# The query stack of a two-stream decoder kernel comes back as 96 rows, and six rows behind it as a second transfer where they must be zero

## The chip, the cores and the metric

The kernel runs on one core of one Trainium2 chip. The metric is the device time of one execution in microseconds (us); lower is better. A core has a matrix engine (TensorE, PE in the profile), a vector engine (VectorE, DVE), a scalar engine (ScalarE, ACT), GpSimd (POOL), a queue engine that only issues transfers and waits (SyncE, SP), and 16 DMA engines that move the bytes of every transfer.

## The reference

The reference is a decoder of four layers over `x` of shape (8, 256, 128): eight sequences of 256 tokens with 128 features. Each layer adds a self-attention, a cross-attention over `ctx` and a feed-forward part to `x`, so there are twelve blocks, numbered 0 to 11 in the kernel:

```
0 L0_attn   1 L0_xattn   2 L0_ffn
3 L1_attn   4 L1_xattn   5 L1_ffn
6 L2_attn   7 L2_xattn   8 L2_ffn
9 L3_attn  10 L3_xattn  11 L3_ffn
```

Five of them (1, 4, 6, 7, 9) are attentions with 16 heads of 8 features. Cut to what matters here, each computes for every head

```
scores = q @ k.T / sqrt(8)            # 256 x 256, block 4 adds a relative-position term
attn   = normalised weights(scores)   # block 1: squared relu; the others: softmax
out    = attn @ v
```

with masks of different kinds. In blocks 6 and 7 the kernel subtracts the row maxima of the scores before the exponential.

## The kernel before, in words

The eight sequences are two streams (`s`) of four items each (`ITEMS = 4`); item `k` of block `n` has the number `j = n * ITEMS + k`. The two streams share all engines. Each engine's program is a set of generators, one per stream and a second one per stream that runs ahead ("front" work: projections and the stacks below), and a string of turns written out by hand (`TURNS`) fixes in which order each engine takes steps from them. The order of instructions on every engine is therefore fixed; only waits decide when they run. SP's program is one such order too: an instruction on SP that waits holds back everything behind it, of both streams.

A head has only 8 features, and the matrix engine wants many rows. For the five blocks 1, 4, 6, 7 and 9 (`FRONTS`) the kernel splits q and k into bf16 pieces and stacks six combinations of them: `COMBOS = 6` times 8 features is 48 rows for an even head and 48 for the odd head of the pair, so a stack has `AUG = 96` rows for 8 pairs of heads and 256 tokens, 4,096 bytes per row. The pieces lie in SBUF in another layout than the matrix engine needs. They are sent to a DRAM tensor `s.via[k]` and come back in the wanted layout:

- `stack_out` waits until the pieces are cut (`s.cut`), and writes them to `via` in two transfers of 192 KB (`stacks<-region` in the profile). 
- `stack_back` waits until both have landed (`s.stack_out`) and reads the stack into SBUF. For the queries (`q_back`, k = 0) this is one transfer of 102 rows into `qs` or, in odd items, into `qv` or another room (`qs<-stacks`, `qv<-stacks`, 408 KB). For the keys (`k_back`, k = 1) it is two transfers of 48 rows into the two halves of `kz` (`kz<-stacks` or `region<-stacks`, 192 KB each). Block 4 has a third stack (k = 2) of 96 rows with one transfer back into `qv_of` (384 KB).

Rows 96 to 101 of the query tile belong to the subtracted maxima. `via[0]` has six more rows behind its 96; they are written once with zeros by `zero_rows` (`stacks<-qs`, two transfers of 24 KB) and never again. In blocks 6 and 7 the scores are first computed with rows 96 to 101 at zero, then SP writes the (negated) maxima into these rows (L2872 `dma(qs[AUG:AUG + 6, ...], s.mpT, s.m_stack)`, `qs<-mpT`), and the scores are computed again. The key tile holds ones in these rows in blocks 6 and 7, and in the odd items of block 9, which use the room of block 6. In blocks 1 and 4 the key tile holds zeros there.

In every front but block 4's the order on SP is: q out, q back, k out, k back. In block 4 it is: third stack out and back, q out, k out, then q back and k back directly behind each other. Block 4 also sends its relative-position scores through DRAM to shift each row by its own offset (`skew<-region`, `skew_room<-skew`, `P<-skew`, L2829 and L2848).

The matrix engine waits for the stacks in `stacks_in` (L802), and in block 4 in `L1_xattn`: first for the third stack, then for everything. All transfers back raise `s.stack_in` by 16 each. `back_before(j)` is the count that all earlier items have raised; SP itself waits for it before it overwrites `via` (L2693).

Of the kernel before, what the change touches and what calls it, by code (L numbers as in the profile page):

```python
# [32 lines left out]
AUG = COMBOS * 2 * DH  # L33
# [486 lines left out]
def program(nc, dram, where, out):  # L520
# [153 lines left out]
    ITEMS = B // 2  # L674
# [22 lines left out]
    def out_before(j):  # L697
        return before(j, 2, 1)
# [19 lines left out]
    def stacks_of(j):  # L718
        return 3 if j // ITEMS == 4 else 2

    def back_before(j):

        m = FRONT_SEQ.index(j)
        return 48 * m + 16 * min(max(m - ITEMS, 0), ITEMS)

    UNITS = [(f, k) for f in range(FT) for k in range(2)]

# [14 lines left out]
    def tensor_program(e):  # L742
        p = Hand(e, "tensor")
# [58 lines left out]

        def stacks_in(s, j):
            yield
            p.wait_ge(s.stack_in, back_before(j) + 16 * (stacks_of(j) + 1))
            p.wait_ge(s.f_out, out_before(j) + 2)
            p.wait_ge(tables, IDENTB)

# [171 lines left out]
        def L0_xattn(s, b, j):  # L980
            yield from stacks_in(s, j)
            p.wait_ge(s.mask_ready, j % ITEMS + 1)
            yield from attend(s, j, s.maskT_of[j % 2], True)
            yield from finish(s, j, W1["L0x_o"], None)
# [144 lines left out]
        def L1_xattn(s, b, j):  # L1129
            qs, qv, kz, v = s.qs_of[4][j % 2], s.qv_of[j % 2], s.kz_of[4][j % 2], s.v_of[4][j % 2]  # L1130
            yield
            p.wait_ge(s.stack_in, back_before(j) + 16)
            p.wait_ge(s.f_out, out_before(j) + 2)
            p.wait_ge(place_sem, 64)
# [36 lines left out]
            for h in range(H + 7):  # L1171
                if h < H:
                    yield from shift(h)
                now = h - 5
                if 0 <= now < H:
                    yield
                    p.wait_ge(s.stack_in, back_before(j) + 64)
                    p.clear(s, "S0")
                    for t in range(TOK):
                        o = s.S0[:, t * S:(t + 1) * S]  # L1180
                        mm(o, qs[:, now // 2, t * 128:(t + 1) * 128], kz[:, now % 2, now // 2, :], True, False)
                        i = mm(o, identb[:, :], L1x_mask[:, t, :], False, True)
                    i.then_inc(s.to_vector, 1)
                    p.fill(s, "S0", s.heads_out)
                if now - 2 >= 3 and (now - 2) % 4 == 3:
                    yield from weigh(now - 2)
                if 0 <= now - 1 < H:
                    yield from turn(now - 1)
                yield
# [219 lines left out]
        def L2_attn(s, b, j):  # L1409
            yield from stacks_in(s, j)  # L1410
            p.wait_ge(scalar_tables, BANDS)
            yield from score_maxima(s, j, bands[:, 0:2, :], 96, 160)
            yield from put_maxima(s)
            yield from attend(s, j, bands[:, 2:4, :], False, 96, 160)
            yield from finish(s, j, P["L2a_o"], RW["L2a_ob"])

        def L2_xattn(s, b, j):
            yield from stacks_in(s, j)
            p.wait_ge(s.mask_ready, ITEMS + j % ITEMS + 1)
            yield from score_maxima(s, j, s.mask_of[j % 2], 0, S)  # L1420
            yield from put_maxima(s)
            yield from attend(s, j, s.maskT)
            yield from finish(s, j, P["L2x_o"], RW["L2x_ob"])
# [1252 lines left out]
    def sync_program(e):  # L2676
        d = Hand(e, "sync")

        def dma(dst, src, sem):
            d.e.dma_start(dst, src).then_inc(sem, 16)  # L2680
# [19 lines left out]
        def stack_back(s, j, k, dsts, clean):  # L2700
            yield
            d.wait_ge(s.stack_out, d.now(s.stack_out))
            d.wait_ge(skew_zero, 160 if j < 2 * ITEMS else 288)
            d.wait_ge(consts_sem, QV_ZERO[s.n])
            d.wait_ge(s.rooms_clean, clean)
            rows_back = s.via[k].rearrange("(r m) -> r m", m=PAIRS * S)
            at = 0
            for dst in dsts:
                n = dst.shape[0]
                dma(dst.rearrange("p i s -> p (i s)"), rows_back[at:at + n], s.stack_in)  # L2710
                at += n

        def q_back(s, j):
            yield from stack_back(s, j, 0, [s.qs_of[j // ITEMS][j % 2][0:AUG + 6]], 0)

        def k_back(s, j):
            yield from stack_back(s, j, 1, [s.kz_of[j // ITEMS][j % 2][HALF * par:HALF * (par + 1), par] for par in range(2)],
# [2 lines left out]
        def front(s, b, j):  # L2720
# [15 lines left out]
            if n == 4:  # L2736
                yield
                d.wait_ge(place_sem, 64)
                yield from stack_out(s, j, 2)
                yield from stack_back(s, j, 2, [s.qv_of[j % 2][0:AUG]], ROOMS[4][1] if j % 2 else 0)  # L2740
                yield from stack_out(s, j, 0)
                yield from stack_out(s, j, 1)
                yield
                d.wait_ge(s.heads_out, H * (ITEMS + k))
                d.wait_ge(s.stack_in, back_before(j) + 16)
                yield from q_back(s, j)
                yield from k_back(s, j)
            else:
                yield from stack_out(s, j, 0)
                yield from q_back(s, j)  # L2750
                yield from stack_out(s, j, 1)
                yield from k_back(s, j)
# [246 lines left out]
```

## Time and profile before

| | |
|---|---|
| runs of the kernel | 2109.3, 2112.57, 2112.61 us; median 2112.57 us |
| span of the profiled execution, first to last instruction | 2089.2 us |
| profiled execution's own time | not recorded; the median of the runs is 23.4 us more than the span |
| PE busy / DVE / ACT / POOL | 1735.3 / 1437.8 / 1036.7 / 461.8 us |
| mean share of the 16 DMA engines | 35.9% hardware queues, 1.4% GpSimd's queue |
| mean granted clock of the matrix engine | 0.929 of full |

The times of single instructions and transfers come from one profiled execution. "Busy" is the time in which an engine ran at least one instruction. The chain of waits is followed back from the last instruction: at each step to whatever released it.

### The profile page before, as it was taken

Reading aid. Unit: us, or ns where it says so; the run is one execution under the profiler, and the core shown is the slowest. Engines: PE = TensorE matmul, PEld = TensorE weight load, DVE = VectorE, ACT = ScalarE, POOL = GpSimd, SP = SyncE. Lnnn points to the kernel's source line nnn. Section 1 sums busy time; section 2 is a strip of 40 time slices with the busy share of each in tenths; the row PEclk is TensorE's granted clock in tenths of the full one; section 3 lists DMA queues with packets and bytes.
Section 4 is the critical chain, followed back from the end, with each engine's and each line's share of the span. In section 5 each row is a group of like instructions: output and inputs, shape, how many; then the busy total and the mean of one; then the engine's idle time right before and its main releaser. Section 6 shows DMA issues by size and latency. Waiting matters only on the chain.

```text
span 2089.2 us, 39934 instructions
## 1 busy us (share of the span) xinstructions
PE 1735.3 (83%) x14536; PEld 1346.3 (64%) x14536; DVE 1437.8 (69%) x4894; ACT 1036.7 (50%) x2588; POOL 461.8 (22%) x448
## 2 busy tenths in 40 slices
PE   6588999999998477778999688899978966774886
PEld 5455687777766355556888576766647865553785
DVE  6688624777877477688988766777875456567743
ACT  3277524666765456657433354445533444541443
POOL 3300110000002000000455400000165554413452
PEclk9899999999999689899999899999988989985998
DMA  5234068000000878878200323323205643322456
GB/s 179 72 82 116 19 217 255 1 1 1 1 1 12 261 207 239 231 204 235 82 1 1 88 72 91 86 70 81 64 25 168 198 138 95 91 75 105 133 179 203
DMA packets 210603, 228.95 MB, mean 110 GB/s; under 512 B 15508, under 2 KB 178732, under 8 KB 209768
## 3 DMA queue, kind: packets, MB, share of 16 engines
q1 hardware_dynamic: 205416, 216.10, 35.9%
q0 software_dynamic: 4992, 10.30, 1.4%
q8 instruction: 116, 1.90, 0.4%
q14 instruction: 79, 0.65, 0.1%
HBM read 130.96 MB, written 94.98 MB: 108 GB/s over the span
## 4 chain that ended last, share of the span: by engine, by line
PE 47%; DVE 22%; DMA 13%; ACT 6%; POOL 5%; issue 4%; SPq 2%; DVEq 0%; ACTq 0%; POOLq 0%
PE banks L746 41%; DMA stacks<-region 3%; ACT P L1512 3%; PE banks L1061 3%; DMA back<-mask,block_to 2%; SPq L2680 2%; POOL sorted L2568 2%; DVE region L1918 2%; DMA skew<-region 2%; DVE P L1838 2%; DVE negm L1849 2%; DVE route L1838 1%; DVE P L2090 1%; ACT region L1512 1%; DVE region L1838 1%
## 5 line engine op out<-in xcount | busy, mean ns | idle before, releaser
L2504 POOL TENSOR_TENSOR norms<-norms,consts 128x2 f32<-128x2 f32 x112 | 81.7, 731 | 1235.5 <-DVE norms L1842 1235.2
L1512 ACT ACTIVATE P<-P,negm 128x256 f32<-128x256 f32 x512 | 240.7, 498 | 118.6 <-DVE negm L2110 64.6
L1512 ACT ACTIVATE P<-banks 128x512 f32<-128x512 f32 (+2 forms) x392 | 187.8, 511 | 158.7 <-PE banks L746 157.0
L1849 DVE TENSOR_REDUCE negm<-banks 128x2 f32<-128x512 f32 (+1 forms) x264 | 148.7, 590 | 31.8 <-PE banks L746 28.6
L746 PE MATMUL banks<-kz,qs 128*128 128x256 bf16 (+1 forms) x512 | 124.7, 279 | 33.6 <-DMA kz<-stacks 16.3
L1512 ACT ACTIVATE region<-banks 128x384 f32<-128x384 f32 (+4 forms) x221 | 108.7, 506 | 77.1 <-PE banks L746 56.5
L746 PE MATMUL banks<-xnT,region 128*128 128x256 f32 x544 | 139.0, 389 | 3.6 <-ACT xnT L1512 3.5
L746 PE MATMUL banks<-bands,identb 128*128 128x160 bf16 (+1 forms) x768 | 140.2, 244 | 0.0
L746 PE MATMUL banks<-region 64*128 64x256 f32 (+6 forms) x922 | 126.3, 364 | 9.0 <-ACT region L1512 3.3
L746 PE MATMUL banks<-qs,kz 128*128 128x256 bf16 (+2 forms) x512 | 113.1, 264 | 22.1 <-DMA kz<-stacks 8.4
L746 PE MATMUL banks<-qv,region 128*128 128x256 bf16 (+2 forms) x512 | 112.7, 262 | 15.6 <-ACT P L1512 13.3
L746 PE MATMUL banks<-kz,region 128*128 128x256 f32 x512 | 121.7, 384 | 4.0 <-DVE skew_room L1838 2.8
L2583 POOL DMA_INDIRECT back<-mask,block_to x92 | 89.4, 972 | 107.9 <-DVE mask L2338 99.2
L746 PEld LDWEIGHTS banks<-xnT,region 128*128 128x128 f32 x544 | 99.2, 193 | 21.8 <-ACT xnT L1512 7.6
L746 PEld LDWEIGHTS banks<-kz,region 128*128 128x128 f32 x512 | 95.6, 191 | 19.9 <-DVE skew_room L1838 4.9
L1838 DVE TENSOR_TENSOR P<-P 128x512 f32<-128x512 f32 (+1 forms) x136 | 84.6, 662 | 33.4 <-ACT P L1512 32.5
L746 PEld LDWEIGHTS banks<-region 128*128 128x128 f32 (+3 forms) x922 | 80.4, 162 | 36.8 <-issue 16.4
L746 PE MATMUL banks<-P,region 128*32 128x256 f32 (+6 forms) x1408 | 91.7, 321 | 9.9 <-ACT P L1512 3.7
L746 PE MATMUL banks<-region,identb 128*128 128x256 bf16 x384 | 99.9, 287 | 0.0
L2110 DVE CUSTOM_DVE_ANT_0 P<-banks,region 128x256 f32<-128x256 f32 x256 | 92.6, 418 | 9.4 <-PE banks L746 9.4
L746 PE MATMUL banks<-region,qv 128*128 128x256 bf16 (+2 forms) x384 | 78.7, 267 | 23.7 <-ACT region L1512 9.8
L1153 PE MATMUL banks<-perm,P 128*128 128x128 f32 x512 | 81.8, 289 | 17.5 <-DVE region L2160 9.1
(288 smaller groups left out, 4462.0 us busy)
## 6 DMA issues: line engine op xcount, KB each, us to landing
stacks<-region SPq DMA_DIRECT2D x178, 192.0 KB, 3.0
sorted<-qs SPq DMA_DIRECT2D x4, 4160.0 KB
skew<-region SPq DMA_DIRECT2D x64, 256.0 KB, 4.0
qs<-stacks SPq DMA_DIRECT2D x24, 408.0 KB
kz<-stacks SPq DMA_DIRECT2D x48, 192.0 KB
skew<-region SPq DMA_DIRECT2D x64, 128.0 KB, 3.3
skew_room<-skew SPq DMA_DIRECT2D x32, 256.0 KB, 3.8
P<-skew SPq DMA_DIRECT2D x32, 256.0 KB, 3.6
```

The lines of the kernel that those rows point to most:

```text
L746: return p.e.matmul(o, lhsT, rhs, start=start, stop=stop)
L1061: i = p.e.transpose(s.T[:, k * S + t * 128:k * S + (t + 1) * 128], s.P[:, n // 2 % 2, n % 2, t, k * 128:(k + 1) * 128], ident)
L1153: m = p.e.transpose(s.T[:, k * S + t * 128:k * S + (t + 1) * 128], s.P[:, i % 2, 0, t, k * 128:(k + 1) * 128], ident)
L1512: return a.e.activation(o, i, f, **kw)
L1838: return v.e.tensor_tensor(o, a, b, op)
L1849: return v.e.tensor_reduce(o, a, AX, op, negate=negate)
L1918: step(v.e.tensor_copy(dst, t.unsqueeze(1).to_broadcast([128, dst.shape[1], S])))
L2110: m = v.e.tensor_tensor_reduce(Pq[:, t, :], s.bank[par][:, t * S:(t + 1) * S], rel[:, h, 128 - 128 * t:128 - 128 * t + S], -1.0, 3.0e38, A ...
L2504: g.e.tensor_tensor(room[:, :, 0], room[:, :, 0], pows[:, :], ALU.pow).then_inc(done, 1)
L2568: g.e.indirect_dma_start(s.sorted_x[w][:, :], place(s, item, k, t), s.own_rows[:, item, t, :], None).then_inc(s.moved[item % 2], 16)
L2583: g.e.indirect_dma_start(s.back[:, :], to, s.block_y[:, n % 2, :], None).then_inc(s.stored[n % 2], 16)
L2680: d.e.dma_start(dst, src).then_inc(sem, 16)
```

## The change

The query stack comes back as 96 rows everywhere. In blocks 6, 7 and 9 a second transfer follows it at once, for rows 96 to 101. In blocks 1 and 4 rows 96 to 101 of the query tile are no longer written. The counts follow: an item raises `s.stack_in` by 48 in block 1 and by 64 in the four others.

```
     def back_before(j):
         m = FRONT_SEQ.index(j)
-        return 48 * m + 16 * min(max(m - ITEMS, 0), ITEMS)
+        return 48 * m + 16 * max(m - ITEMS, 0)
...
         def stacks_in(s, j):
             yield
-            p.wait_ge(s.stack_in, back_before(j) + 16 * (stacks_of(j) + 1))
+            p.wait_ge(s.stack_in, back_before(j) + (48 if j // ITEMS == 1 else 64))
...
         def q_back(s, j):
-            yield from stack_back(s, j, 0, [s.qs_of[j // ITEMS][j % 2][0:AUG + 6]], 0)
+            qs = s.qs_of[j // ITEMS][j % 2]
+            yield from stack_back(s, j, 0, [qs[0:AUG]] + ([qs[AUG:AUG + 6]] if j // ITEMS in (6, 7, 9) else []), 0)
```

`stack_back` issues one transfer for each tile of its list, one behind the other, with no wait between them.

## Rows read from the trace of the kernel before

**Rows 1.** The page: span, first line of busy time, chain by engine.

```profile
span 2089.2 us, 39934 instructions
...
PE 1735.3 (83%) x14536; PEld 1346.3 (64%) x14536; DVE 1437.8 (69%) x4894; ACT 1036.7 (50%) x2588; POOL 461.8 (22%) x448
...
PE 47%; DVE 22%; DMA 13%; ACT 6%; POOL 5%; issue 4%; SPq 2%; DVEq 0%; ACTq 0%; POOLq 0%
```

**Rows 2.** Busy time by window; last three: PE clock, DMA share, GB/s.

```profile
672.00:990.00 318.00, 232.20 (x1898) 160.75 (x1898) 233.83 (x807) 186.63 (x435) 15.69 (x19) 0.86 0.81 227
1150.00:1490.00 340.00, 296.69 (x3368) 229.11 (x3367) 243.16 (x606) 162.47 (x360) 30.90 (x36) 0.95 0.31 79
...
777.40:783.40 6.00, 5.19 (x30) 2.92 (x22) 0.97 (x3) 1.07 (x3) 0.00 (x0) 0.50 0.84 240
```

**Rows 3.** The page's DMA issues: count, KB each.

```profile
qs<-stacks SPq DMA_DIRECT2D x24, 408.0 KB
...
qv<-stacks SPq DMA_DIRECT2D x4, 384.0 KB
```

**Rows 4.** DMA view of 1156:1162 us, 40 slices of 0.15 us: busy tenths, GB/s.

```profile
DMA  0000003703132232334424244424210000004999
GB/s 0 0 0 0 0 0 82 82 27 55 55 55 82 109 137 109 164 164 164 164 109 164 109 164 164 164 109 164 109 55 27 0 0 0 0 0 106 201 177 174
```

**Rows 5.** DMA view of 750:755 us, 40 slices of 0.125 us: GB/s.

```profile
GB/s 172 135 205 242 348 336 234 156 238 369 393 328 238 139 164 98 164 197 66 164 328 360 393 360 393 328 66 33 33 0 0 0 0 0 0 70 193 188 180 172
```

**Rows 6.** DMA busy tenths of 771:785 us, then of 940:952 us, 40 slices each.

```profile
DMA  3078997958768689999999999999444445658879
...
DMA  8986999999958899999994599999998444436999
```

**Rows 7.** Pieces of the chain of waits: start us, us, what.

```profile
171.90 6.14 DMA kz<-stacks
...
709.22 7.21 DMA skew<-region
...
777.39 6.00 DMA skew<-region
...
784.85 6.84 DMA skew<-region
...
863.52 5.57 DMA P<-skew
...
944.90 5.88 DMA skew_room<-skew
...
1191.30 4.74 DMA qs<-mpT
...
1212.20 2.48 DMA qs<-mpT
...
1288.79 6.10 DMA qs<-mpT
```

**Rows 8.** SP's issues in order of time: start us, us, what.

```profile
1288.44 0.26 SPq L2680 DMA_DIRECT2D qv<-stacks  x1
1288.79 0.79 SPq L2680 DMA_DIRECT2D qs<-mpT  x1
...
1744.37 0.27 SPq L2680 DMA_DIRECT2D qs<-stacks  x1
1747.92 1.24 SPq L2680 DMA_DIRECT2D stacks<-region  x2
1751.48 0.78 SPq L2680 DMA_DIRECT2D kz<-stacks  x2
```

**Rows 9.** Issues that touch stacks: ns min/median/max, first and last start us.

```profile
L2680 SPq DMA_DIRECT2D stacks<-qs x2: 402/536/670, 35.7 to 39.5; - x2
```

**Rows 10.** The chain at 1751 us: start us, us, what.

```profile
1751.83 3.33 DMA kz<-stacks
```

**Rows 11.** PE's waits: us in total, times, longest us.

```profile
PE banks L746 <- DMA kz<-stacks: 24.7, 6, 11.5
```

## The prediction

> **What bounds the kernel now.** I read the page first: the chain of waits is matrix engine 47%, vector engine 22%, transfers 13%, and the matrix engine is busy for 1735.3 of 2089.2 us [rows 1]. So the whole is bound by the matrix engine's fixed order, and a transfer counts only where the chain runs through one. The windows show where that is [rows 2]: in block 4 (672 to 990 us) the 16 DMA engines are busy for 0.81 of the time, in blocks 6 and 7 (1150 to 1490 us) for 0.31. The list of issues says what the change can touch: 102-row transfers of 408 KB [rows 3]. There are 40 of them (24 into `qs`, 16 into `qv`), of which 24 belong to blocks 6, 7 and 9 and 16 to blocks 1 and 4.
>
> Then the transfer itself. From 1156 to 1162 us the 102 rows travel alone [rows 4]. For 25 slices of 0.15 us, 3.7 us in all, the share stays at 2 to 4 tenths and the rate does not pass 164 GB/s. Six of 16 engines are 0.375, so the rows lie on about six engines, 17 rows each: 4,096 bytes at 164 / 6 = 27 GB/s are 0.15 us a row, 2.6 us for 17. The trace also has the shape of the new transfer: block 4's third stack is 96 rows, 384 KB, at four places into `qv` [rows 3] and at four into another room. One is under way at the end of the busy part of 750 to 755 us, and it runs at 328 to 393 GB/s [rows 5], the rate of all 16 engines. 393 KB at 360 GB/s are 1.1 us, 6 rows per engine. So 96 rows need 1.5 us less than 102, and 11 rows or 1.65 us less on each of the six engines that carried 17.
>
> **What the change removes.** The gain is that work of other transfers no longer queues behind 17 rows on six engines. In the DMA view this shows as a tail: the share falls to 4 tenths for some time while the last rows drain. Such a tail ends just where a chain piece ends. The piece that starts at 777.39 us and takes 6.00 us ends at 783.4, after a tail of 2.1 us (780.8 to 782.9); the one at 944.90 ends at 950.8, as a tail of 1.5 us ends [rows 6, 7]. Five chain pieces of block 4 and one of block 1 read this way; their tails are 1.2 to 2.5 us, the longest before the end of the piece at 709.22. Spread over 16 engines the same bytes take 6/16 of a tail, so 10/16 of it goes.
>
> - Block 4, no second transfer there: pieces at 709.22, 777.39, 784.85, 863.52 and 944.90 us [rows 7]. Tails of 2.5, 2.1, 1.8, 1.5 and 1.5 us make 9.4 us; 10/16 are 5.9 us.
> - Block 1, no second transfer either: the piece at 171.90 us has a tail of 1.25 us, so 0.8 us. At the start both streams send 17 rows within 2.3 us of each other; I put 1 us there, by the same measure. Together 1.8 us.
> - Blocks 6 and 7: three pieces are the 24 KB of maxima, `qs<-mpT`, and their six rows go to the same few engines. Undisturbed this takes 2.48 us; right behind 102-row transfers it takes 4.74 and 6.10 us [rows 7]. For the first, two such transfers were issued 5 us before; they lose 20 of 34 rows, 3.0 us, more than the 2.3 us of excess, so I take 2. For the second one transfer is issued 0.35 us ahead [rows 8]: 10 of 17 rows go (six stay, one is the new transfer's), 1.5 us.
> - Block 9: chain pieces there land in 2.9 to 3.3 us, as undisturbed ones do. Nothing to win.
>
> The sum is 5.9 + 1.8 + 3.5 = 11.2 us if every piece passes its gain on.
>
> **What it adds.** 24 transfers of six rows, 24 KB. On the DMA engines one row each on six of them, 0.15 us: already in the counts above. On SP an issue each. The nearest row is the same shape in the other direction, `stacks<-qs`, 402 to 670 ns; a 102-row issue takes 0.26 to 0.27 us when SP is not crowded; the dearest neighbour is the six-row `qs<-mpT`, which walks 48 source rows, at 0.79 us [rows 8, 9]. I take 0.3 us, since the new transfer has six whole rows like the first two and not the source of the third. All 24 would be 7.2 us (6.2 to 19). But what stands behind them on SP? At 1744.37 us nothing: the next issue comes 3.5 us later because its pieces are not cut [rows 8]. Nearly all places in block 9 and most in 6 and 7 look like this. At 1288.44 us the maxima's transfer stands right behind, and it is on the chain: 0.3 us there, and about as much at two or three places more, of which I count one. Cost on the chain 0.6 us (0.3 to 4).
>
> The wait of `stacks_in` for blocks 6, 7 and 9 is for 64 and not 48. Its last part is still the key stack, which is issued some 7 us after the query's [rows 8], so the second transfer has landed long before. Two transfers behind each other to one semaphore exist already: the keys' pair at 1751.48 us is landed 3.33 us after the first was handed over [rows 10], so the second of a pair costs a few tenths and not a landing of its own.
>
> The Trainium skill speaks against the change here: its page "DMA: Bandwidth & Descriptors", section "Rules for kernel authors", says to coalesce small transfers, as under 64 KB mostly overhead is paid, and the section on one DMA's anatomy gives 2.0 us of fixed cost each. By that the 24 additions would cost 48 us if each were waited for alone. The trace disagrees for pairs issued together, by its 3.33 us for the keys' two.
>
> **The sum.** 11.2 less 0.6 is 10.6 us. That is too much to expect: the chain follows one path, while two streams share the engines in fixed order, and with one wait shorter the matrix engine meets the next. Two facts bear on how much survives. The matrix engine really stands still for the key stacks only in part: 24.7 us over six times, of which 11.5 at 708 us, where the DMA engines are full and a tail is short [rows 11]. And while the chain runs through a transfer in block 4 the matrix engine is often at work for the other stream: busy 5.19 of 6.00 us from 777.4 us [rows 2]. I take 0.6 of it, between all and a quarter: 6.5 us. The change lies wholly inside the span: 2089.2 would become 2082.7, and the median of 2112.57, which is 23.4 us above the span, 2106.0 us, 0.3% less.
>
> **The rivals.**
>
> *All of it arrives.* The shifting loop of block 4 is a ring of transfers and exponentials in which each stream waits for its own last lane, so nothing else need take a delay's place: minus 10 to 15 us, about 2100. For it: the ends of the tails and of the pieces match. Against it: the busy matrix engine in the same windows.
>
> *Hidden.* The tails delay only the stream that is behind, and the vector engine (22% of the chain) is next at once. Then a quarter or less of 10.6 us survives, minus 0 to 3, about 2110.5. For it speaks again 5.19 of 6.00 us busy; against it that the granted clock is 0.50 there [rows 2], the lower level of 1.2 GHz, after stretches in which the engine stood waiting.
>
> *The clock.* In block 4 the mean granted clock is 0.86 and it falls to 0.50 for stretches of 6 to 12 us [rows 2]. An earlier arrival changes which gaps it follows. One such stretch more or less is 3 to 6 us of matrix work either way. This moves each of the other cases and gives the ends of the range.
>
> *SP's issues: the slower side.* The added issues cost as much as the maxima's, 0.79 us, and most stand on the chain, because SP's order is shared: what one stream issues late, the other waits for. 24 times 0.79 is 19 us, less the 6.5 us gained: plus 12, 2125. It needs more than (6.5 + 4.2) / 24 = 0.45 us of chain per added issue to come out slower at all. Against it stands the gap behind nearly each of them [rows 8].
>
> *The change does not do what it says:* 96 rows also go to few engines. The 328 to 393 GB/s of the same shape exclude it [rows 5].
>
> **Chances.** Forecast (minus 4.3 to minus 10) 0.45; all of it 0.17; hidden, within 4.2 us, 0.29; slower by SP's issues 0.04 and by the clock 0.05. A measurement of this kernel tells about 0.2%, 4.2 us, from no change (its three runs lie within 3.3 us). So faster 0.62, same 0.29, slower 0.09. The range reaches over most of the first two cases and the hidden one, to 2097 and 2114.
>
> **What the profile after would show.** A query transfer alone at 300 GB/s or more for about 1.1 us; no tails of 4 tenths in block 4 except where six-row transfers run; the pieces near 777, 785, 863 and 945 us shorter by about 1 us each; `qs<-mpT` behind a query transfer at about 3 and 4.5 us; SP's issues of 24 KB near 0.3 us; 24 more of them. If tails go and the end of block 4 (near 990 us) does not come earlier, the hidden case holds. If block 4 gains and the blocks 6 to 9 give it back, SP's issues are the cause. The prediction would be wrong above all by the surviving share, 0.6, and by the clock.

## The result

| | us |
|---|---|
| before, four runs | 2109.3 to 2115.41, median 2112.59 |
| changed, four runs | 2091.02 to 2096.54, median 2094.55 |
| ratio, 95% interval | 0.9913 [0.9898, 0.9927] |
| forecast | 2106.0, range 2097 to 2114 |

The changed kernel is 18 us faster, 0.87%. The direction was right, but the gain is nearly three times the forecast and the time lies below the range.

The profile after shows a puzzle first. Its page:

```profile
span 2094.5 us, 39958 instructions
## 1 busy us (share of the span) xinstructions
PE 1745.7 (83%) x14536; PEld 1356.6 (65%) x14536; DVE 1438.9 (69%) x4894; ACT 1035.9 (49%) x2588; POOL 461.7 (22%) x448
```

Its span is 5.3 us longer than that of before [rows 1], although its runs are 18 us shorter. The profiled execution of the changed kernel took 2096.31 us at a span of 2094.5: only 1.8 us lie around a span. By that, an estimate, the first profile of before was not an execution of 2112 us with 23.4 us around it, as I had read it, but one of about 2091 us, quicker than each of its four timed runs. Below, the same kernel is profiled again and spans 2103.4 us. Spans of single profiles can't carry a difference of 0.9% here. Sections of them can, where they agree.

The trace of every kernel here holds 5,232 records of the vector engine, those that the page does not count as busy among them, in the same order. So the records with the numbers 445, 1,561, 2,435, 3,560 and 4,523, counted from nought, mark the same work in each. They cut the execution at 240, 672, 990, 1490 and 1850 us of the first profile: start and block 1; blocks 2 and 3; block 4; blocks 5 to 7; blocks 8 and 9 and what lies between; the last. Durations of these sections in us, worked out from the traces of all 14 profiles:

```
                       1      2,3    4      5-7    8,9    10,11
before, first          240.2  431.7  318.1  500.0  360.1  238.8
before, again  (e1)    242.0  431.7  318.6  503.4  363.1  244.5
changed, first         237.7  431.7  306.8  498.3  366.4  253.3
changed, again (e2)    238.4  431.7  311.7  500.7  366.4  247.6
e3  96 in 1, 4         236.4  431.7  305.3  500.5  364.2  244.1
e4  split in 6, 7, 9   240.5  431.7  321.0  500.4  361.4  242.1
e5  96 in 4            241.2  431.7  306.7  505.0  364.1  248.2
e6  96 in 1            236.9  431.7  316.1  504.7  364.5  247.6
e7  112 everywhere     236.6  431.7  312.2  501.1  365.2  246.2
e8  96 or 112          235.6  431.7  305.5  499.3  364.1  244.2
e9  100 in 4           240.2  431.7  310.8  506.9  367.4  249.0
e10 111 in 4           241.9  431.7  339.5  499.5  363.8  248.4
e11 V as 64 + 32       237.5  431.7  308.8  499.0  363.1  249.5
e12 V as 68 + 28       236.6  431.7  320.6  499.0  366.4  246.6
```

Blocks 2 and 3 have none of these transfers and take 431.7 us in all 14. Block 4 separates: 316.1 to 321.0 us in the four profiles with 102 rows there, 305.3 to 311.7 in the five with 96 rows and nothing else changed in it. The last section, which the change doesn't touch, spreads from 238.8 to 253.3 us, and the first profile of before has the shortest of all, as it has of blocks 8 and 9 (360.1 us). Between the two first profiles the first four sections gain 15.5 us together, and the last two lose 6.3 and 14.5. That is the puzzle solved as far as it concerns the change: the quick end of one profile, from block 8 on, hid a gain in block 4.

Block 4 in the changed kernel, as a window (last three: clock, DMA share, GB/s):

```profile
669.40:976.20 306.80, 228.30 (x1898) 159.28 (x1898) 233.48 (x807) 186.42 (x436) 15.81 (x19) 0.87 0.84 235
```

Against [rows 2] the same 1,898 matrix instructions are busy for 228.3 us instead of 232.2, and the engine is idle for 78.5 us instead of 85.8. The 11.2 us between these two profiles are 7.3 us of idle time and 3.9 us of busy time, with a granted clock of 0.87 and 0.86. The DMA share rose, from 0.81 to 0.84: hardly fewer bytes in less time, and on more engines at once.

The transfer alone, in slices of 0.15 us from 1142 us (two issues, 96 rows and six):

```profile
DMA  0000000029791549999120000000000000000006
GB/s 0 0 0 0 0 0 0 0 82 164 109 300 27 164 164 410 437 437 382 27 55 27 0 0 0 0 0 0 0 0 0 0 0 0 0 0 0 0 0 133
```

By the GB/s it takes 14 slices from first to last, 2.1 us, where the 102 rows took 25 [rows 4], and reaches 437 GB/s where they stopped at 164. In block 4 the stretches of 4 tenths have shrunk to a slice or two (763 to 777 us, then 917 to 929 us; compare [rows 6]):

```profile
DMA  0998992000989994999999789999999999999989
...
DMA  9999999999999898999999999999940067995999
```

Over the whole of block 4, cut into slices of 0.25 us, the packets in the traces fill 0.30 to 0.45 of the 16 engines for 18.75 to 20.5 us in the four profiles with 102 rows, and for 5.25 to 6.75 us in the five with 96.

The list of issues, and SP's issues in order of time in block 9:

```profile
qs<-stacks SPq DMA_DIRECT2D x24, 384.0 KB
...
qs<-stacks SPq DMA_DIRECT2D x12, 24.0 KB
qv<-stacks SPq DMA_DIRECT2D x12, 24.0 KB
```

```profile
1733.83 0.68 SPq L2680 DMA_DIRECT2D qs<-stacks  x2
1737.84 1.25 SPq L2680 DMA_DIRECT2D stacks<-region  x2
```

Both issues together take 0.68 us where one took 0.27 [rows 8], and the next thing SP does still comes 3.3 us later. The issue of six rows by itself takes 0.33 us in the median.

The chain of waits after, in block 4 and at two transfers of maxima:

```profile
705.25 5.35 DMA skew<-region
712.17 6.03 DMA skew<-region
...
785.83 4.79 DMA skew_room<-skew
...
852.79 5.41 DMA P<-skew
...
917.49 6.23 DMA kz<-stacks
929.69 5.73 DMA skew<-region
...
1198.60 2.48 DMA qs<-mpT
...
1276.27 4.28 DMA qs<-mpT
```

Most of these pieces are not those of [rows 7]: the chain takes other transfers. SP's order is the same in both kernels, so each piece of [rows 7] has its counterpart after, and the raises of its semaphore in the traces say when it landed. From issue to landing in us, with the second profile of each kernel (e1 and e2) beside the first:

| piece of before | before, e1 | after, e2 | difference of the means | forecast |
|---|---|---|---|---|
| block 1, 171.90 | 6.14, 6.10 | 3.87, 3.72 | -2.3 | -0.8 |
| block 4, 709.22 | 7.21, 6.97 | 5.35, 5.45 | -1.7 | -1.6 |
| 777.39 | 6.00, 6.02 | 3.98, 3.66 | -2.2 | -1.3 |
| 784.85 | 6.84, 6.83 | 2.39, 2.24 | -4.5 | -1.1 |
| 863.52 | 5.57, 6.69 | 5.41, 4.55 | -1.2 | -0.9 |
| 944.90 | 5.88, 6.37 | 6.71, 6.94 | +0.7 | -0.9 |
| maxima, 1191.30 | 4.74, 6.38 | 2.67, 2.69 | -2.9 | -2 |
| maxima, 1288.79 | 6.10, 6.15 | 4.28, 4.35 | -1.8 | -1.5 |

The 2.48 us at 1198.60 is the counterpart of the undisturbed piece at 1212.20 [rows 7]; the first maxima's counterpart was issued at 1178.16 us and is no longer on the chain. The matrix engine's waits for the key stacks fell from 24.7 us over six [rows 11] to:

```profile
PE banks L746 <- DMA kz<-stacks: 15.1, 4, 9.3
```

### The profile page after: what moved, and what is told of

Same layout as the page of the kernel before. It is cut to its first block, busy times and chain, and to the rows that moved or that the text cites. A ratio compares the mean times of both kernels' runs of the same rounds, so it can differ in the third digit from the quotient of the medians.

```text
span 2094.5 us, 39958 instructions
## 1 busy us (share of the span) xinstructions
PE 1745.7 (83%) x14536; PEld 1356.6 (65%) x14536; DVE 1438.9 (69%) x4894; ACT 1035.9 (49%) x2588; POOL 461.7 (22%) x448
## 4 chain that ended last, share of the span: by engine, by line
PE 49%; DVE 22%; DMA 11%; ACT 7%; issue 6%; POOL 2%; SPq 2%; another core or an unknown queue 0%; DVEq 0%; ACTq 0%; POOLq 0%
PE banks L746 42%; ACT P L1512 4%; PE banks L1061 3%; DMA stacks<-region 3%; SPq L2680 2%; DVE region L1918 2%; DMA back<-mask,block_to 2%; DVE P L1838 2%; DVE negm L1849 2%; DVE P L2090 1%; ACT region L1512 1%; DVE route L1838 1%; DVE region L2160 1%; DVE region L1838 1%; PE banks L1153 1%
```

## The experiments

Ratios are to the kernel before on the same chip, with 95% intervals. Its median was 2109.84 us beside e1 to e4, 2107.74 beside e5 to e8 and 2114.05 beside e9 to e12.

**Is the gain real, and is the first profile typical?** e1 is the kernel before, e2 the changed one, both unchanged.

> The kernel before, unchanged, timed against itself and profiled again. Its first profile spans 2089.2 us although its runs take 2109 to 2115 us, while the changed kernel's profile spans 2094.5 us and its runs take 2091 to 2097. Theory A (the imbalance of the 102-row transfers costs real time, and the first profile shows an execution that is quicker than the usual one): the runs take about 2112 us again and a profile of the same chip spans about 2110 us. Rival B (the kernel before has two ways to run, 2091 and 2112 us, and the change only alters how often each comes): some runs or the profile come out near 2091 us. Rival C (the two sets of runs stood under different conditions): ratio to itself 1.000 either way.

> The changed kernel once more beside the kernel before on one chip. A: 2094 us, ratio 0.991. B: some runs near 2110 us. C: ratio nearer to 0.997, as predicted.

e1: 2110.19 us, ratio 1.0001 [0.9981, 1.002], profile 2103.4 us; its 12 runs lie between 2102.57 and 2113.21. e2: 2090.89 us, ratio 0.9903 [0.9873, 0.9933], profile 2096.7 us. The gain stands, and rivals B and C fall: the runs of before spread over 17 us without two groups (23 of them, 2098.74 to 2115.94), and none came as low as the 2091 us of its first profile. As A said, that execution was quicker than the usual one; why is not known beyond the two sections in which it was, blocks 8 and 9 and the last.

**Which blocks?** e3 and e4 halve the change, e5 and e6 halve e3. The lists `NARROW` and `SECOND` name the blocks with 96 rows and with the second transfer:

```
+            n, qs = j // ITEMS, s.qs_of[j // ITEMS][j % 2]
+            yield from stack_back(s, j, 0, [qs[0:AUG] if n in NARROW else qs[0:AUG + 6]]
+                                  + ([qs[AUG:AUG + 6]] if n in SECOND else []), 0)
# e3: NARROW (1, 4), SECOND ()      e4: both (6, 7, 9)
# e5: NARROW (4,),   SECOND ()      e6: NARROW (1,), SECOND ()
```

The counts in `back_before` and `stacks_in` follow the two lists.

> Only blocks 1 and 4 get the 96-row transfer (16 of 40), blocks 6, 7 and 9 keep one transfer of 102 rows. By my sum block 1 and 4 hold 7.7 of 11.2 us: with the whole at minus 18 us this gives about minus 12 us, ratio 0.994. Rival (the gain sits where the six-row maxima stand behind the query transfer, blocks 6 and 7): minus 3 us or less.

> Only blocks 6, 7 and 9 are changed: 96 rows and the six-row transfer behind them; blocks 1 and 4 keep 102 rows. If the parts add up, this and the run with blocks 1 and 4 alone sum to about minus 18 us, with minus 6 us here (ratio 0.997). If the added issues cost on the chain, it is 0 or slower here. Rival: minus 12 us or more here, the gain is in the maxima.

> Block 4 alone gets 96 rows (8 of 40 transfers). Aligned by the vector engine's instruction count, the profiles put 11 us of the gain into block 4. Theory (real relief of the full DMA engines): minus 13 to 16 us in the runs, ratio 0.993, and a gain of about 11 us between 672 and 990 us of the profile. Rival (the gain is made of small shifts everywhere and not of block 4): minus 3 us.

> Block 1 alone gets 96 rows (8 of 40). My prediction had 1.8 us at best there; the profiles say about 3. Both: ratio 0.998 to 0.999, span up to 240 us shorter by 2 to 4 us. Rival (an early gain is handed on and grows in block 4 by another alignment of the streams): minus 8 us or more.

| | us | ratio | less than before |
|---|---|---|---|
| e3, blocks 1 and 4 | 2089.95 | 0.9910 [0.9881, 0.9939] | 19.0 |
| e4, blocks 6, 7, 9 | 2105.58 | 0.9986 [0.9965, 1.0007] | 3.0 |
| e5, block 4 | 2095.88 | 0.9939 [0.9915, 0.9962] | 12.9 |
| e6, block 1 | 2104.14 | 0.9983 [0.9971, 0.9995] | 3.6 |

(The last column is one less the ratio, times the median of before.) The parts add up within their intervals: 12.9 + 3.6 + 3.0 is 19.5, the whole in e2 20.5. Block 4, a fifth of the transfers, has two thirds of the gain. I had expected 12 us of e3 and 6 of e4. In blocks 6, 7 and 9 the interval reaches from 7.4 us of gain to 1.5 of loss, so these runs do not show that the change does anything for the time there.

**Is it the number of engines or the number of bytes, and do the issues cost?** e7 takes the other way to 16 engines: 112 rows, more bytes, one transfer. e8 does so only where the zeros are needed.

```
-        self.via = nc.dram_tensor(f"stacks{n}", (3, (AUG + 6) * PAIRS * S), BF16).ap()
+        self.via = nc.dram_tensor(f"stacks{n}", (3, (AUG + 16) * PAIRS * S), BF16).ap()
...
-            yield from stack_back(s, j, 0, [s.qs_of[j // ITEMS][j % 2][0:AUG + 6]], 0)
+            yield from stack_back(s, j, 0, [s.qs_of[j // ITEMS][j % 2][0:AUG + 16]], 0)     # e7
+            n = j // ITEMS                                                                   # e8
+            yield from stack_back(s, j, 0, [s.qs_of[n][j % 2][0:AUG + (16 if n in (6, 7, 9) else 0)]], 0)
...
-            dma(s.via[0, AUG * PAIRS * S:]..., s.qs[0:6]..., skew_zero)
+            dma(s.via[0, AUG * PAIRS * S:]..., s.qs[0:16]..., skew_zero)
```

> All 40 query transfers carry 112 rows (96, the six, and ten more rows of zeros): seven rows on each of 16 engines, one transfer, no added issue, but 448 KB where 408 KB were. If the count of engines is the cause: as fast as the changed kernel, 2091 to 2094 us, a little slower in block 4 for 16 more rows. Rival (fewer bytes and rows are the cause): no gain or slower than before.

> 96 rows in blocks 1 and 4, 112 rows in one transfer in blocks 6, 7 and 9. It has the gain of blocks 1 and 4 and no added issue. If the six-row transfers cost something in the changed kernel: 2 to 4 us faster than it, 2088 us. If not: the same within the noise.

e7: 2090.67 us, 0.9920 [0.9894, 0.9946]. 10% more bytes per transfer than before, and all of the gain within the interval: it is not the bytes. e8: 2087.59 us, 0.9916 [0.9890, 0.9942]. Its median is the lowest of all kernels here, but its interval is nearly the changed kernel's, so the 24 added issues cost nothing that can be seen, and e8 is an equal, not a better version. These intervals are 11 us wide: the 0.6 us that I had forecast for the issues is far below what they could show.

**How does the cost grow?** e9 and e10 change block 4's query transfer alone, to 100 and to 111 rows (the room behind `via` as in e7).

```
+            n = j // ITEMS
+            yield from stack_back(s, j, 0, [s.qs_of[n][j % 2][0:111 if n == 4 else AUG + 6]], 0)    # e9: 100
```

> Only block 4's query transfer is changed, to 100 rows, 400 KB. If such a transfer costs the rows of its fullest engine: 100 rows lie on 10 engines with 10 rows each, against 17 (102 rows) and 6 (96 rows, minus 11.9 us in the runs and 10.4 in the profiles). 7 of 11 rows of relief: minus 7 to 8 us, ratio 0.9965. Rival (it is the whole or nothing: all 16 engines or not): 0. Rival (bytes: 2 of 6 rows fewer): minus 4 us.

> Block 4's query transfer carries 111 rows, 444 KB, which lie on three engines with 37 rows each: 20 more on the fullest than 102 rows have. By the same slope, 1.1 us per row, plus 22 us in the runs, ratio 1.010, all of it between 672 and 990 us. Rival (a transfer of the query lies beside other waits and only its 9% more bytes count): within 3 us of the kernel before. Sharper than the slope if the three engines become the bound of block 4.

e9: 2106.24 us, 0.9962 [0.9947, 0.9976]: 8.0 us less, expected 7 to 8. e10: 2134.03 us, 1.0096 [1.0071, 1.0122]: 20.3 us more, expected 22. The engines' counts in the expectations are those by which the Trainium skill, page "DMA: Bandwidth & Descriptors", section "Why a DMA increments its semaphore by 16 and not by 1", splits a transfer: over the largest number up to 16 that divides its outermost size, so 16 for 96 and 112, 10 for 100, 6 for 102, 3 for 111. No view names the engine of a packet, but the traces confirm the counts in another way: they hold every raise of a semaphore by a transfer. In each of block 4's eight items `s.stack_in` goes up by 64, in 64 raises with 96 or 112 rows, 59 with 100, 55 with 102 and 52 with 111. The third stack and the two key transfers make 48 of them. The query's is left with 16, 11, 7 and 4: one for each engine, and one more for the rest of the 16 where the engines are fewer. Likewise e12's two parts of 68 and 28 rows leave 20, which is 5 and 15.

The time follows the row count of the fullest engine that this gives. The last column is the difference, divided by the difference in rows and by eight transfers:

| rows | on the fullest engine | block 4, us | against 102 rows | per row and transfer |
|---|---|---|---|---|
| 96 | 6 | 307.2 (mean of five) | -11.3 | 0.128 |
| 100 | 10 | 310.8 | -7.7 | 0.138 |
| 102 | 17 | 318.5 (mean of four) | | |
| 111 | 37 | 339.5 | +21.0 | 0.131 |

One row takes 0.15 us on one engine by [rows 4], so 0.85 to 0.92 of each row stands in block 4's time. 112 rows (e7, seven on each) should give 308.2 and have 312.2 in one profile, which is as far off as the five of 96 rows lie from each other. The same holds for the one profile of 100 rows: 310.8 us lies inside the 305.3 to 311.7 of 96. Its runs exclude the rival of no gain (5.1 to 11.2 us less), but not that 100 rows are as good as 96, for e5's interval is 8.0 to 17.9.

In e10 the chain goes through the transfers that queue behind the long one, and they are long (the first of these, `stacks<-region`, is on the chain of before too, with 7.23 us):

```profile
700.37 11.03 DMA stacks<-region
713.27 9.96 DMA kz<-stacks
...
795.79 9.52 DMA P<-skew
...
878.05 9.39 DMA P<-skew
...
946.63 10.25 DMA kz<-stacks
```

and its block 4 as a window shows what a mean hides:

```profile
673.60:1013.10 339.50, 234.51 (x1898) 165.00 (x1898) 233.84 (x807) 187.12 (x436) 15.81 (x19) 0.83 0.77 214
```

The DMA share is the lowest of the three, 0.77, in the kernel that suffers most from its transfers; the matrix engine stands idle for 105.0 us. The tail of three engines shows: the packets fill 0.2 to 0.3 of the 16 engines for 29 us of block 4, where the nine profiles with 96 or 102 rows have 3.5 to 5.75.

**Does it need to be the query's transfer, and what does an issue cost there?** e11 and e12 are the changed kernel with block 4's third stack in two parts. The counts in `back_before` and in three waits follow (80 for 64, 32 for 16).

```
-                yield from stack_back(s, j, 2, [s.qv_of[j % 2][0:AUG]], ROOMS[4][1] if j % 2 else 0)
+                yield from stack_back(s, j, 2, [s.qv_of[j % 2][0:64], s.qv_of[j % 2][64:AUG]], ...)   # e11
+                yield from stack_back(s, j, 2, [s.qv_of[j % 2][0:68], s.qv_of[j % 2][68:AUG]], ...)   # e12
```

> The changed kernel, with block 4's third stack brought back as 64 and 32 rows, all 16 engines each, six rows per engine as before: eight more issues on SP and nothing else. Theory: an issue beside other work costs nothing that can be seen or at most 0.3 us each, 0 to 2.4 us over the changed kernel, ratio to the kernel before 0.991 to 0.992. Rival (a second transfer costs a landing of its own, 2 us): plus 16 us, ratio 0.998.

> The same with 68 and 28 rows: 68 rows lie on four engines with 17 rows each, 28 on 14 with two each. 13 more rows on the fullest engines of a transfer that the matrix engine waits for, eight times, about 2 us each: up to plus 15 us over the run with 64 and 32, by the slope of 1.1 us per row plus 14. Rival (the imbalance matters only for transfers queued behind the query's): plus 3 us or less.

e11: 2094.27 us, 0.9910 [0.9889, 0.9932], where the changed kernel has 0.9903 in e2: eight more issues cost nothing seen, and a landing of its own is excluded. e12: 2100.02 us, 0.9935 [0.9911, 0.9959], so 5.7 us over e11; the two intervals overlap. Block 4 of its profile is 11.8 us longer, 320.6 against 308.8, and 8.9 longer than the longest of the five with an even split (311.7). The direction is as expected, same bytes, same issues, other rows per engine; of the size, 14 us expected, the runs show less than half and the profile most. One profile each and this spread don't settle which.

The third stack is waited for directly. Waits of the matrix engine in block 4, e12:

```profile
PE banks L746 <- DMA qv<-stacks: 12.2, 2, 10.9
...
PE banks L912 <- ACT OTp L1512: 9.2, 6, 6.4
```

and e11:

```profile
PE banks L746 <- DMA kz<-stacks: 9.7, 2, 9.0
PE banks L746 <- DMA qv<-stacks: 9.3, 1, 9.3
```

The waits for the third stack have grown by 2.9 us in total and those of L912, 4.7 us in e11, by 4.5. Where the rest of the 11.8 us stands these lines don't show.

## Why the prediction was wrong

**Right: what the transfer does.** 102 rows on six engines, 96 on 16, 1.65 us less on each of the six. The raises of the semaphore and the four row counts (0.13 us per row, against 0.15 from [rows 4]) bear it out. That a transfer of six rows behind it is cheap was right too: 0.33 us per issue (0.3 forecast), time to spare behind it on SP in block 9, nothing measurable in e7 and e8. The advice of the Trainium skill, page "DMA: Bandwidth & Descriptors", section "Rules for kernel authors", to coalesce small transfers was no reason against the change here. The 2.0 us of fixed cost that the prediction took from the same page stand in its section "Anatomy of one DMA — SWDGE (gpsimd) path", so for transfers that GpSimd issues and not SP; 24 times that did not show. The maxima's two transfers, forecast at about 3 and 4.5 us, took 2.67 and 4.28.

**Wrong: the size of block 4's term.** "Five chain pieces", their visible tails, "10/16 of it goes": 5.9 us, and after the factor of 0.6 some 3.5. Measured are 11.3 us in the profiles and 12.9 in e5's runs. Two steps failed. The first is the count. I took 9.4 us of tails, those at the ends of five pieces of the chain; 19.4 us of such stretches stand in block 4 with 102 rows and 6.0 with 96. So 13.4 us of them went, 1.7 for each of the eight transfers, which is the 1.65 us of my own text. The product of the two, 13.2 us, I never made, and 0.86 of it arrived. The second is the factor: 10/16 of the 13.4 us would be 8.4, and the block gained 11.3. Why it gained more than the tails give by that factor is not shown; the shorter busy time of the matrix engine, 3.9 us of the 11.2, may be part of it. The table of counterparts says the same: of the five pieces one was over in 2.3 us instead of 6.8, where I had 1.1 us of gain, and one did not become shorter at all. Nor do pieces of one chain bound a term: the second profile of the same kernel takes its chain through other transfers.

**Wrong: the surviving share of 0.6.** I took it from the matrix engine being at work for the other stream in the same windows. The gain of block 4 in the runs, 12.9 us, is not less than that in its own section, 11.3, and of the plain product 0.86 arrived. A likely reason, which no run tests apart, is that both streams wait on the same queue in turn, each for its own round trips through DRAM, so that the other stream's work does not fill the wait. The rival "all of it arrives" had this mechanism, with a sum of 10.6 us that was itself too small.

**Too small: block 1.** The term was 1.8 us before the factor; the profiles have 241.0 us (mean of six with 102 rows) against 237.0 (mean of eight with 96 or 112), 4.0 us, and e6's runs 3.6. The one piece of the chain that I had there gained 2.3 us, not 0.8. The 4.0 us are 0.3 of eight times 1.65: there a good part is hidden, and still more than the two tails that I counted arrived.

**Not settled: blocks 6, 7 and 9.** Forecast was 3.5 less 0.6 us; e4 gives minus 3.0 [-7.4, +1.5]. The two disturbed transfers of maxima became shorter by 2.1 and 1.8 us in the first profiles, as forecast. The section of blocks 5 to 7 lasts 499.5 us in the mean of the five profiles with the second transfer in it and 502.9 in the seven with 102 rows, 3.4 less, as forecast; but the two groups overlap (498.3 to 500.7, 499.5 to 506.9), and blocks 8 and 9 have 0.8 us more. It points to a gain and doesn't show one. With 11.3 us of block 4 and 4.0 of block 1 these make 17.9 of the 18 us.

**Wrong: what lies around the span.** I added 23.4 us to the span. It is 1.8 us; the profiled execution was simply quicker than the runs. The forecast as a difference didn't depend on it, but it should have warned that one profile of this kernel may be 20 us from its median.

The rivals: the slower side, by SP's issues, did not occur; "hidden" is excluded for block 4 by e5. The clock did its part: in block 4 the same 1,898 matrix instructions are busy for 3.9 us less, at a granted clock of 0.87 instead of 0.86, which is of the size that I gave one stretch at the lower level. It probably follows from the shorter waits, but no run separates it. Over whole spans the mean granted clock of the 14 profiles lies between 0.921 and 0.936.

## What to carry to other kernels

Count the rows of the fullest DMA engine and not the bytes: of a transfer's outermost size ask into how many equal parts up to 16 it divides, and prefer 96 and a small second transfer, or 112 with padding, to 102. The raises of the transfer's semaphore in a trace tell the count. Where queues are full, as in block 4, price an imbalance by rows saved times time per row times transfers, and count the tails of the whole stage and not those at the ends of chain pieces; where they are not, as in block 1, this is an upper bound. A lower mean share of the DMA engines can belong to the slower kernel. Before one trace is read for its span, compare the profiled execution with the timed runs, and cut several profiles at the same instructions to see which sections repeat.

## What the runs showed that I had not expected

A section without these transfers repeats to 0.1 us in 14 profiles (431.7 us, blocks 2 and 3), while the last one, with its experts' gathers and scatters through DRAM, spreads over 14.5 us (238.8 to 253.3) in kernels that are alike there. That these gathers and scatters are the cause is not shown. The scatter of whole runs, 17 us for the kernel before, is of that size.

The cost of an uneven split fits one line from six to 37 rows on the fullest engine, at 0.13 us per row of 4,096 bytes. The scatter of 5 to 6 us between profiles of alike kernels leaves room for a bend between six and ten rows.
